# An early-fusion block on one Trainium2 core: the drain of a hand-ordered pipeline rewritten, more tile sets, and the last pair's norm in groups

## The chip, the core and the metric

The kernel runs on one NeuronCore of a Trainium2 chip. Five engines each have their own instruction stream and meet only at semaphores: PE (TensorE), DVE (VectorE), ACT (ScalarE), POOL (GpSimd) and SP (SyncE, which issues the DMAs here). The metric is device time of one execution in microseconds, the median of the runs. The kernel before took 1186.11 us, median of three runs from 1184.85 to 1186.3.

## The reference

The input is 32 images of 3x224x224 and 32 texts of 128x192. Each image becomes 196 tokens of 192 channels, beside one class token; with its text that makes 325 rows. Attention and a feed-forward network (FFN) follow. Cut to what matters:

```
def forward(x, ...):                                   # tokens of one image
    loc = dwconv(gelu(conv(x, pl_w, pl_b, stride=16)), pl_dw, pl_pw, pl_pwb)   # layer L
    g = gelu(conv(wavelet_packet(x), pg_w1, pg_b1))
    glob = conv(gelu(dwconv(g, pg_dw, pg_pw, pg_pwb)), pg_w2, pg_b2)           # layer G
    h = (1 - gate) * loc + gate * glob
    h = relu(dwconv(h, f1_...)); h = relu(dwconv(h, f2_...))                   # F1, F2
    t = layernorm(dwconv(loc + h, f3_...)) * ln_g + ln_b                       # F3
h = concatenate([cls, t, txt])                         # 1 + 196 + 128 rows of 192
n = layernorm(h)
q, k, v = (gelu(n @ w1 + b1) @ w2 + b2 for each of the three)
s = q @ k.T / SCALE * mask          # row i sees rows i-63 .. i; no softmax
h = h + layernorm(s @ v) * ln_w + ln_b
def bitlinear(x, w, g):             # x to 8 bits per row, w to -1, 0, 1
    x = rmsnorm(x, g); return round8(x) @ ternary(w).T
up, gate = split(bitlinear(layernorm(h), w_in, g_in))  # 192 -> 2 x 512
h = h + bitlinear(silu(gate) * up, w_out, g_out)       # 512 -> 192
```

Here dwconv is a depthwise 3x3 convolution followed by a matrix over the channels.

## The kernel before

Two images form a pair, and 16 pairs, 0 to 15, flow through a software pipeline of 23 turns (lines quoted are those of the kernel before). In turn `it` the engines embed pair it-1, compute its layers L, F1 and F2 as pair it-2, its F3 and token norm as pair it-3, the attention inputs as pair it-4, the attention's output norm and the FFN's input scales as pair it-5, and FFN tiles as pairs it-6 and it-7. A function `turn` for each engine lists the steps by hand, in one order for all turns; in the turns at the end, flags (`on[...]`) drop the steps for which no pair is left, and what is left keeps its order. An engine takes its instructions strictly in that order.

A depthwise layer is split by channels: nine taps over one part of them on DVE (L1349, L1359), nine products on ACT (L953) and their sums on POOL (L1905 to L1923) for the rest, then matmuls on PE (L474 to L479; for F3 L706 and L708). `add_loc` (L1378) takes F2's result and makes the input of F3; `token_biased` (L1389) takes F3's result. Attention has transposes on PE, six MLP layers (L528 to L539), scores, and products with the values; then the output norm of pair f: statistics on DVE (`output_bn`, L1439), six centred tiles on ACT (`output_norm`), one product and one sum over all tiles on POOL (`output_gain`, L1943; `output_add`, L1952).

The FFN works on tiles of 128 rows, five per pair; pairs 11 and 15 have a sixth with the rows left over. The steps of a tile, in order: transposes on PE (L627), copy to `xq` on ACT (L1016), hidden matmuls into two PSUM banks `up` and `gate` on PE (L638), tanh on ACT (`gate_tanh`, L1022), two products on DVE (`gated`, L1524, and `lifted`, L1544), the gain on POOL (L1889), a sum of squares on ACT, a maximum and five small instructions on DVE (`hidden_round`, L1308 to L1321) with a root on POOL (L1894, L1882), rounding on ACT (`round_hidden`, L1002), four transposes on PE (L648), copy to `yq` on ACT (L1010), the output matmuls on PE (L658), one instruction into `o_sb` on DVE (`finished`, L1534) and a store from SP.

Two PSUM banks and one set of scratch (`th`, `ya`, `y_f`, `yg` and so on) serve all tiles in turn; only for the last pair, `side(f, n)` gives odd tiles a second set, whose banks and memory earlier stages have left by then:

```
return n % 2 if last(f) else 0
```

`ffn_in` waits until DVE has read the previous tile's two banks, and until the tile before that has its output. `o_sb` has two buffers. The attention scratch and `x_sb`, `w_emb` and `early` are reused as tile scratch at the end, so rows of the trace name a tile's `ya` or `s` by the tensor whose memory it takes.

The steps of other lines that the prediction names: input layer norm on ACT (L967), token layer norm (DVE L1389 to L1398 and POOL L1985, L1995), the FFN's input gain on DVE (`token_gain`, L1490) and input rounding on ACT (L996).

Of the kernel before, what the change touches and what calls it, by code (L numbers as in the profile page):

```python
# [9 lines left out]
ALU = mybir.AluOpType  # L10
# [105 lines left out]
def stores_before(g, parity):  # L116
    return 16 * sum(stores_of(*TILE_LIST[i]) for i in range(parity, g, 2))


def side(f, n):  # L120

    return n % 2 if last(f) else 0


def alone(f, n):

    return last(f) and n > 0


def build(nc, xt, txt, cls, squares, f3w, v2w, plw, w1w, haar, cols, broads, gout, win, wout, mask,  # L130
          ident, out):
    ctx = ExitStack()
    with ctx:
# [80 lines left out]
        dq2 = [sb(f"dq2_{i}", [P, 1]) for i in range(2)]  # L214
        o_sb = [sb(f"o_sb{i}", [P, D]) for i in range(2)]
# [9 lines left out]
        ups, gts = [pUP, pA], [pGT, pB]  # L225
# [4 lines left out]
        ths, yas, yfs, sqs = ([a[:, :], x_flat[:, i * HID:(i + 1) * HID]] for i, a in enumerate((th, ya, y_f, sq_f)))  # L230
        ygs, r2s = ([a[:, :], e_flat[:, i * HID:(i + 1) * HID]] for i, a in enumerate((yg, r2)))
        xqs = [xq[:, :, :], e_flat[:, 2 * HID:2 * HID + P].bitcast(BF16).rearrange("p (c n) -> p c n", c=2)]
        yqs = [yq[:, :, :], e_flat[:, 2 * HID + P:2 * HID + 3 * P].bitcast(BF16).rearrange("p (c n) -> p c n", c=4)]
        s2s = [s2[:, :], e_flat[:, 2 * HID + 3 * P:2 * HID + 3 * P + 8]]
# [33 lines left out]
        y_scaled, h2_ready = sem("y_scaled"), sem("h2_ready")  # L268
        f1s = sem("f1s")
# [7 lines left out]
        stored = [sem("stored0"), sem("stored1")]  # L277
# [87 lines left out]

        CELLS = [(img, t, (P, ROWS[2])[t]) for img in range(2) for t in range(2)]
# [16 lines left out]
        def _(sp):  # L383
# [6 lines left out]
            def store(f, n):  # L390
                at = tile_no(f, n) % 2
# [14 lines left out]
            def join(f, par):  # L406
                sp.wait_ge(h2_ready, f + 1)
# [59 lines left out]
        def _(pe):  # L467
# [149 lines left out]
            def rounded_token_transposes(f, n):  # L617
# [13 lines left out]
            def ffn_in(f, n):  # L631
                m, s = rows_of(f, n), side(f, n)
                pe.wait_ge(f_xq, tile_no(f, n) + 1)
                if not (first(f) and n < 2 or alone(f, n)):
# [17 lines left out]
            def ffn_out(f, n):  # L652
                m, s = rows_of(f, n), side(f, n)
                pe.wait_ge(f_yq, tile_no(f, n) + 1)
                if not (first(f) and n == 0 or alone(f, n)):
# [209 lines left out]

            pe.wait_ge(s_early, ALL_EARLY)
# [13 lines left out]
            all_turns(turn)  # L880
# [3 lines left out]
        def _(act):  # L884
# [119 lines left out]
            def rounded_hidden(f, n):  # L1004
                m, s = rows_of(f, n), side(f, n)
                act.wait_ge(f_tr2, tile_no(f, n) + 1)
                if not (first(f) and n == 0 or alone(f, n)):
# [64 lines left out]
            def turn(it, par, on):  # L1072
# [80 lines left out]
                if on[5]:  # L1153
                    output_norm(it - 5, 0)
# [6 lines left out]
                if on[5]:  # L1161
                    output_norm(it - 5, 1)
# [120 lines left out]

            act.wait_ge(s_early, ALL_EARLY)
# [7 lines left out]
            all_turns(turn)  # L1292
# [3 lines left out]
        def _(dve):  # L1296
            v = nc.vector

            def hidden_round(j, f, n, par):
# [4 lines left out]
                if j == 0:  # L1304
                    dve.wait_ge(f_yg, tile_no(f, n) + 1)
                    if not (first(f) and n == 0 or alone(f, n)):
# [212 lines left out]

            def gated(f, n):  # L1520
# [6 lines left out]
            def finished(f, n):  # L1527
# [3 lines left out]
                at = tile_no(f, n) % 2  # L1531
                if not (first(f) and n < 2):
# [650 lines left out]
```

## Time and profile before

| what | value |
|---|---|
| median of three runs | 1186.11 us |
| profiled execution, own time | 1183.86 us |
| its span in the trace | 1182.1 us |
| mean granted TensorE clock | 0.94 of full |
| PE busy | 1056.5 us (89%) |
| DVE busy | 968.8 us (82%) |
| ACT busy | 883.8 us (75%) |
| POOL busy | 796.2 us (67%) |

The span runs from the first to the last instruction or transfer of the profiled execution; 1.76 us of its own time lie around it. Shares of busy time are means over the ramp, the steady turns and the drain, which differ. A line number in a row is one of the kernel before; a clock of 1.00 is full speed of TensorE. A row says which engine, the line, the operation, and out<-in by the program's names.

### The profile page before, as it was taken

Reading aid. Unit: us, or ns where it says so; the run is one execution under the profiler, and the core shown is the slowest. Engines: PE = TensorE matmul, PEld = TensorE weight load, DVE = VectorE, ACT = ScalarE, POOL = GpSimd, SP = SyncE. Lnnn points to the kernel's source line nnn. Section 1 sums busy time; section 2 is a strip of 40 time slices with the busy share of each in tenths; the row PEclk is TensorE's granted clock in tenths of the full one; section 3 lists DMA queues with packets and bytes.
Section 4 is the critical chain, followed back from the end, with each engine's and each line's share of the span. In section 5 each row is a group of like instructions: output and inputs, shape, how many; then the busy total and the mean of one; then the engine's idle time right before and its main releaser. Section 6 shows DMA issues by size and latency. Waiting matters only on the chain. (4 is left out here: it accounts for less than half of the span.)

```text
span 1182.1 us, 18959 instructions
## 1 busy us (share of the span) xinstructions
PE 1056.5 (89%) x5594; PEld 701.3 (59%) x5594; DVE 968.8 (82%) x2799; ACT 883.8 (75%) x2179; POOL 796.2 (67%) x913
## 2 busy tenths in 40 slices
PE   6886999999999999999999999999999877868434
PEld 4664676767666666767575757576766545444211
DVE  1678778989999999999898989899999976754543
ACT  4455767898979797979798988889897856654433
POOL 4246467778787878777877877787878755653422
PEclk9797999999999999999999999999999988979655
DMA  8111010101010101011010101010100000000000
GB/s 331 42 48 41 1 49 3 52 9 59 10 59 7 58 4 64 4 28 41 19 49 12 55 10 59 10 58 11 58 10 18 10 16 5 23 4 17 4 19 15
DMA packets 23686, 41.14 MB, mean 35 GB/s; under 512 B 3648, under 2 KB 20384, under 8 KB 21280
## 3 DMA queue, kind: packets, MB, share of 16 engines
q1 hardware_dynamic: 23584, 39.93, 10.0%
q8 instruction: 46, 0.75, 0.3%
q14 instruction: 56, 0.46, 0.1%
HBM read 31.02 MB, written 7.99 MB: 33 GB/s over the span
## 5 line engine op out<-in xcount | busy, mean ns | idle before, releaser
L1359 DVE SCALAR_TENSOR_TENSOR bank<-padA,c_col,bank 128x406 f32<-128x406 f32 x560 | 358.6, 640 | 9.1
L496 PE MATMUL bank<-x_sb,w_emb 128*128 128x392 f32 x576 | 221.3, 513 | 5.4 <-ACT padA L903 3.1
L953 ACT ACTIVATE prod<-padB,c_col 128x196 f32<-128x196 f32 x432 | 176.5, 451 | 7.2 <-DVE padB L1371 3.9
L1889 POOL TENSOR_TENSOR yg<-y_f,c_gout 128x512 f32<-128x512 f32 (+1 forms) x79 | 100.4, 1271 | 69.2 <-DVE y_f L1544 69.1
L496 PEld LDWEIGHTS bank<-x_sb,w_emb 128*128 128x128 f32 x576 | 102.5, 195 | 63.0 <-issue 12.8
L953 ACT ACTIVATE early<-padB,c_col 128x196 f32<-128x196 f32 x288 | 118.8, 449 | 3.7 <-POOL accB L1923 3.6
L1524 DVE SCALAR_TENSOR_TENSOR ya<-th,bank 128x512 f32<-128x512 f32 (+1 forms) x79 | 54.1, 684 | 56.4 <-ACT th L1022 55.2
L638 PE MATMUL bank<-w_in,xq 128*128 128x512 bf16 (+1 forms) x316 | 86.6, 399 | 8.8 <-ACT xq L1016 8.8
L1010 ACT ACTIVATE yq<-bank 128x512 bf16<-128x512 f16 (+1 forms) x79 | 46.8, 592 | 48.4 <-PE bank L648 47.2
L474 PE MATMUL bank<-accA,w_sq 128*128 128x196 f32 x256 | 67.6, 346 | 10.9 <-POOL accB L1923 6.8
L1022 ACT ACTIVATE th<-bank,sm 128x512 f32<-128x512 f32 (+1 forms) x79 | 53.7, 680 | 29.0 <-PE bank L638 29.0
L528 PE MATMUL bank<-xT,w_sq 128*128 128x325 f32 x192 | 65.7, 453 | 5.4 <-ACT hq L911 3.3
L1908 POOL TENSOR_TENSOR prod<-prod 128x392 f32<-128x392 f32 x48 | 48.8, 1016 | 28.8 <-ACT prod L953 28.7
L1905 POOL TENSOR_TENSOR prod<-prod 128x392 f32<-128x392 f32 x48 | 48.9, 1019 | 26.0 <-ACT prod L953 26.0
L1349 DVE TENSOR_SCALAR bank<-padA,c_col 128x406 f32<-128x406 f32 x80 | 51.0, 637 | 18.1 <-ACT padA L903 15.0
L475 PE MATMUL bank<-accB,w_sq 128*128 128x196 f32 x256 | 65.2, 337 | 0.0
L1002 ACT ACTIVATE r<-yg,s 128x512 f32<-128x512 f32 (+1 forms) x79 | 56.7, 718 | 10.7 <-DVE s L1321 10.6
L1943 POOL TENSOR_TENSOR y_sb<-y_sb,c_row 128x1152 f32<-128x1152 f32 x16 | 42.1, 2633 | 32.1 <-ACT y_sb L976 32.1
L1894 POOL TENSOR_SCALAR s<-s 128x1 f32<-128x1 f32 (+1 forms) x79 | 18.5, 235 | 65.2 <-ACT sq_f L1027 62.6
L638 PEld LDWEIGHTS bank<-w_in,xq 128*128 128x128 bf16 (+1 forms) x316 | 29.0, 101 | 52.6 <-ACT xq L1016 17.9
L967 ACT ACTIVATE xh<-h_sb,nm_a,rs_a 128x192 f32<-128x192 f32 (+1 forms) x144 | 60.1, 482 | 0.0
L648 PE MATMUL bank<-c_id,r 128*128 128x128 f16 (+1 forms) x316 | 32.8, 230 | 29.6 <-DVE y_f L1544 25.4
(276 smaller groups left out, 3030.9 us busy)
## 6 DMA issues: line engine op xcount, KB each, us to landing
x_sb<-xt SPq DMA_DIRECT2D x16, 1176.0 KB, 5.2
out<-o_sb SPq DMA_DIRECT2D x64, 96.0 KB
w_sq<-squares SPq DMA_DIRECT2D x1, 3840.0 KB, 16.4
h_sb<-txt SPq DMA_DIRECT2D x32, 51.8 KB
out<-o_sb SPq DMA_DIRECT2D x32, 48.0 KB
h_sb<-txt SPq DMA_DIRECT2D x32, 44.2 KB
w_in<-win SPq DMA_DIRECT2D x1, 1024.0 KB, 17.6
h<-h SPq DMA_DIRECT2D x16, 48.0 KB, 1.9
```

The costliest lines, as they stand in the source:

```text
L474: mm(dstA[img], w[:, AA, :], chunks[img], start=True, stop=False)
L475: done = mm(dstA[img], w[:, B0A + img, :], chunks[2], start=False, stop=True)
L496: done = mm(pE[:, 0:2 * N_PATCH], w_emb[:, k, m, :], x_sb[:, k, :], start=k == 0, stop=k == KC - 1)
L528: mm(dst[c], w[:, AA, :], src[:, c, :], start=True, stop=False)
L638: done = mm(dst[0:m, :], xqs[s][:, c, 0:m], w_in[:, c, half * HID:(half + 1) * HID], start=c == 0, stop=c == 1)
L953: made = go(grid(prod[ACC[s] ^ 1][:, k, :]), tap_view(padB[min(s, 2)], SIDE, k), ACT.Copy, scale=tapcol(s, 1, k))
L967: done = go(xh[0:m, t, at:at + hi - lo], h_sb[0:m, n, lo:hi], ACT.Identity, bias=nm_a[0:m, n:n + 1], scale=rs_a[0:m, n:n + 1])
L1002: go(r2s[s][0:m, :], ygs[s][0:m, :], ACT.Copy, scale=s2s[s][0:m, 6:7], bias=MAGIC_H).then_inc(r2_ready, 1)
L1022: go(ths[s][0:m, :], gts[s][0:m, :], ACT.Tanh, scale=sm[par][0:m, 2, n:n + 1]).then_inc(f_th, 1)
L1359: v.scalar_tensor_tensor(grid(acc if k == TAPS - 1 else run), tap_view(pad, ROWS_A, k), tapcol(s, 0, k), grid(run), ALU.mult, ALU.add).the ...
L1524: v.scalar_tensor_tensor(yas[s][0:m, :], ths[s][0:m, :], 1.0, gts[s][0:m, :], ALU.add, ALU.mult).then_inc(f_y, 1)
L1889: g.tensor_tensor(ygs[s][0:m, :], yfs[s][0:m, :], c_gout[0:m, :], ALU.mult).then_inc(f_yg, 1)
```

## The change

The list of turns ends early, after 17 turns on PE, ACT and SP and 16 on DVE and POOL, and each engine gets a function `drain()` that spells out all its remaining steps, one call a line, in a new order. Up to `finished(11, 0)` on DVE (912.84 us in the trace before) that order is the one of before.

Pairs 13 to 15 are the `TAIL`. `side` lets the tiles of pairs 13 and 14 alternate between two sets of banks and scratch, and those of pair 15 between three; the third set takes the banks pT[0], pT[1] and the memory of `hq`, `hk`, `hv`, `k2`, `xh` and `xT`. In the tail `ffn_in` waits only for the output of the tile that last had the same set. `o_sb`, and the semaphores of its stores, number three instead of two (`OUTS`), for all pairs.

The last pair's output norm and FFN scales are done in three groups of two tiles: statistics, then product and sum on DVE (`last_output`) in place of six instructions on ACT and two on POOL, then the FFN's input statistics, gain and scale, group by group; the roots stay on POOL. Tiles are rounded on ACT as their group is ready, and `join(15)` waits for two of the groups only.

```
+OUTS = 3
+TAIL = PAIRS - 3
 def side(f, n):
-    return n % 2 if last(f) else 0
+    if last(f):
+        return (n + 1) % 3
+    return (tile_no(f, n) - tile_no(TAIL, 0) + 1) % 2 if tail(f) else 0
...
-        ups, gts = [pUP, pA], [pGT, pB]
+        ups, gts = [pUP, pA, pT[0]], [pGT, pB, pT[1]]
...
+        OUT_GROUPS = (slice(0, 2), slice(2, 6, 3), slice(3, 5))
+        TOK_GROUPS = (slice(0, 2), slice(3, 5), slice(2, 6, 3))
...
-        def all_turns(turn):
-            for it in range(PAIRS + DEPTH - 1):
+        def all_turns(turn, stop):
+            for it in range(stop):
...
+            def drain():
...
+                rounded_token_transposes(15, 0)
+                rounded_token_transposes(15, 1)
...
-                if not (first(f) and n == 0 or alone(f, n)):
-                    pe.wait_ge(f_y, tile_no(f, n) * 2)
-                if not (first(f) and n < 2 or last(f) and n == 1):
-                    pe.wait_ge(f_out, tile_no(f, n) - 1)
+                if tail(f):
+                    if side_before(f, n):
+                        pe.wait_ge(f_out, side_before(f, n))
+                    elif side(f, n) == 1:
+                        pe.wait_ge(z_step, (PAIRS - 1) * 4 + 1)
+                    else:
+                        pe.wait_ge(at_act, PAIRS * ACT_UNITS)
+                else:
...
+            def last_output(f, par, j):
...
+                dve.wait_ge(l_root, j + 1)
+                for n in tiles_in(OUT_GROUPS[j]):
+                    m = ROWS[n % TILES]
+                    done = v.scalar_tensor_tensor(y_sb[0:m, n, :], y_sb[0:m, n, :], nm_y[0:m, n:n + 1],
+                                                  row("attn_ln_w", m), ALU.add, ALU.mult)
+                done.then_inc(l_y, 1)
+                dve.wait_ge(l_y, j + 1)
+                for n in tiles_in(OUT_GROUPS[j]):
+                    m = ROWS[n % TILES]
+                    done = v.scalar_tensor_tensor(h2[par][0:m, n, :], y_sb[0:m, n, :], rs_y[0:m, n:n + 1],
+                                                  hb_sb[0:m, n, :], ALU.mult, ALU.add)
+                done.then_inc(l_h2, 1)
...
+            def last_scale_0(f, par, j):
...
+                for n in tiles_in(TOK_GROUPS[j]):
+                    m = rows_of(f, n)
+                    done = v.bn_stats(st_f[0:m, n, :], joint(f, par, n))
...
+            def last_gain(f, par, j):
...
+                v.tensor_reduce(mx_f[:, q], w_g[:, q, :], AXX, ALU.max, apply_absolute_value=True).then_inc(l_f, 1)
...
-                at = tile_no(f, n) % 2
-                if not (first(f) and n < 2):
+                at = tile_no(f, n) % OUTS
+                if not (first(f) and n < OUTS):
```

The order is shown at three places. First POOL, around the last sum of layer F3 of the last pair (out `accB`, on which `token_biased` of pair 15 depends); `y_sb` and `h_1` are the output norm of pair 13, `yg` and `s` FFN tiles. Before:

```order
L1943 TENSOR_TENSOR y_sb<-y_sb,c_row 128x1152
L1952 TENSOR_TENSOR h_1<-y_sb,hb_sb 128x1152
L1905 TENSOR_TENSOR prod<-prod 128x392
L1889 TENSOR_TENSOR yg<-y_f,c_gout 128x512
L1908 TENSOR_TENSOR prod<-prod 128x392
L1911 TENSOR_TENSOR prod<-prod 128x392
L1914 TENSOR_TENSOR prod<-prod 128x196
L1894 TENSOR_SCALAR s<-s 128x1
L1882 TENSOR_TENSOR s<-s,c_mhalf 128x1
L1975 TENSOR_SCALAR sm<-mv_f 128x6
L1882 TENSOR_TENSOR sm<-sm,c_mhalf 128x6
L1923 TENSOR_TENSOR accB<-prod 128x196
```

After:

```order
L3017 TENSOR_TENSOR prod<-prod 128x392
L3020 TENSOR_TENSOR prod<-prod 128x392
L2998 TENSOR_TENSOR yg<-y_f,c_gout 128x512
L3023 TENSOR_TENSOR prod<-prod 128x196
L3067 TENSOR_TENSOR y_sb<-y_sb,c_row 128x1152
L3003 TENSOR_SCALAR s<-s 128x1
L2991 TENSOR_TENSOR s<-s,c_mhalf 128x1
L3076 TENSOR_TENSOR h_1<-y_sb,hb_sb 128x1152
L3032 TENSOR_TENSOR accB<-prod 128x196
```

Before, product and sum of pair 13's output norm stood ahead of all the sums of F3; now they stand between the sums of the products and the sum into `accB`, with a tile's root between them, and two instructions on `sm` (pair 13's FFN scales) are gone from there.

Second DVE, among the last pair's tiles (`x_sb`, `w_emb`, `k`, `hk` and `xT` stand for tile scratch). Before:

```order
L1524 SCALAR_TENSOR_TENSOR x_sb<-x_sb,bank 128x512
L1544 TENSOR_TENSOR x_sb<-x_sb,bank 128x512
L1534 SCALAR_TENSOR_TENSOR o_sb<-bank,dq_0,h_1 128x192
L1308 TENSOR_REDUCE w_emb<-w_emb 128x1
L1311 TENSOR_SCALAR w_emb<-w_emb,sm 128x1
L1314 TENSOR_SCALAR w_emb<-w_emb 128x1
L1317 RECIPROCAL w_emb<-w_emb 128x1
L1318 TENSOR_SCALAR dq_1<-w_emb,c_ws 128x1
L1321 TENSOR_SCALAR w_emb<-w_emb 128x1
L1524 SCALAR_TENSOR_TENSOR ya<-th,bank 128x512
L1544 TENSOR_TENSOR y_f<-ya,bank 128x512
L1534 SCALAR_TENSOR_TENSOR o_sb<-bank,dq_1,h_1 128x192
```

After:

```order
L2167 SCALAR_TENSOR_TENSOR x_sb<-x_sb,bank 128x512
L2187 TENSOR_TENSOR x_sb<-x_sb,bank 128x512
L2167 SCALAR_TENSOR_TENSOR k<-hk,bank 128x512
L2187 TENSOR_TENSOR xT<-k,bank 128x512
L2177 SCALAR_TENSOR_TENSOR o_sb<-bank,dq_0,h_0 128x192
L1855 TENSOR_REDUCE w_emb<-w_emb 128x1
L1858 TENSOR_SCALAR w_emb<-w_emb,sm 128x1
L1861 TENSOR_SCALAR w_emb<-w_emb 128x1
L1864 RECIPROCAL w_emb<-w_emb 128x1
L1865 TENSOR_SCALAR dq_1<-w_emb,c_ws 128x1
L1868 TENSOR_SCALAR w_emb<-w_emb 128x1
```

Before, each tile's two products were followed by the previous tile's output and its own maximum; now the products of two tiles, on two sets, stand in a row, then the output of pair 14's last tile, and only then the maximum of the first of the two.

Third PE, among the last pair's tiles (L627 and L638 are now L697 and L708, L648 and L658 now L718 and L728). Before:

```order
L627 MATMUL bank<-c_id,r 128x128 x2
L638 MATMUL bank<-w_in,w_emb 128x512 x4
L648 MATMUL bank<-c_id,r 128x128 x4
L658 MATMUL bank<-w_out,yq 128x192 x4
L627 MATMUL bank<-c_id,r 128x128 x2
L638 MATMUL bank<-w_in,xq 128x512 x4
L648 MATMUL bank<-c_id,w_emb 128x128 x4
L658 MATMUL bank<-w_out,w_emb 128x192 x4
```

After:

```order
L697 MATMUL bank<-c_id,r 128x128 x4
L708 MATMUL bank<-w_in,w_emb 128x512 x4
L708 MATMUL bank<-w_in,hq 128x512 x4
L718 MATMUL bank<-c_id,r 128x128 x4
L728 MATMUL bank<-w_out,yq 128x192 x4
L697 MATMUL bank<-c_id,r 128x128 x2
L708 MATMUL bank<-w_in,xq 128x512 x4
L718 MATMUL bank<-c_id,w_emb 128x128 x4
L728 MATMUL bank<-w_out,w_emb 128x192 x4
L697 MATMUL bank<-c_id,r 128x128 x2
```

Before, each tile's hidden matmuls were followed by the previous tile's transposes and output; now the input transposes of two tiles and their hidden matmuls stand in a row, and transposes and output of an earlier tile behind them.

## Rows read from the trace of the kernel before

**Rows 1.** The page: span; busy tenths and granted clock in 40 slices.
```profile
span 1182.1 us, 18959 instructions
...
PE   6886999999999999999999999999999877868434
...
PEclk9797999999999999999999999999999988979655
```

**Rows 2.** Busy by stretch: length, then busy us (instructions) of each engine, clock, DMA.
```profile
831.80:894.10 62.30, 61.62 (x345) 41.24 (x344) 58.98 (x175) 53.95 (x134) 49.26 (x56) 1.00 0.10 33
912.80:1182.10 269.30, 181.47 (x948) 110.69 (x946) 166.36 (x546) 150.58 (x346) 132.21 (x151) 0.79 0.05 13
1022.70:1101.80 79.10, 61.57 (x341) 37.93 (x337) 42.81 (x151) 41.24 (x93) 31.98 (x36) 0.89 0.05 14
1108.50:1182.10 73.60, 28.05 (x114) 11.05 (x114) 32.49 (x102) 28.55 (x60) 25.02 (x30) 0.50 0.05 14
```

**Rows 3.** What DVE waited for, 912.8 to 1182.1: total, times, longest.
```profile
DVE ya L1524 <- ACT th L1022: 34.7, 13, 7.2
DVE o_sb L1534 <- PE bank L658: 21.3, 13, 2.9
```

**Rows 4.** Timeline of DVE, four places: start, us, line, op, out<-in.
```profile
912.84 0.42 DVE L1534 SCALAR_TENSOR_TENSOR o_sb<-bank,dq,h 128x192 f32<-128x192 f32 x1
...
1004.07 0.75 DVE L1378 SCALAR_TENSOR_TENSOR padA<-bank,c_gate,locA 128x196 f32<-128x196 f32 x2 [0.98 <-PE bank L479]
...
1022.67 1.15 DVE L1389 TENSOR_TENSOR z_tok<-bank,c_row 128x192 f32<-128x192 f32 x4 [0.63 <-PE bank L708]
...
1101.81 0.61 DVE L1439 BATCH_NORM_STATS2 st_y<-y_sb 128x6 f32<-128x192 f32 x2
```

**Rows 5.** The chain of waits: hidden-layer tiles of the last pair on PE: start, us, what.
```profile
1132.82 1.90 PE bank L638 x4
...
1137.02 0.60 PE bank L648 x4
...
1138.29 0.82 PE bank L658 x4
...
1167.95 1.91 PE bank L638 x4
```

**Rows 6.** Timeline: first transpose of the last pair; the end.
```profile
1131.95 0.40 PE L627 MATMUL bank<-c_id,r 128*128 128x128 f16 x2 [10.48 <-ACT r L996]
...
1177.58 0.41 DVE L1534 SCALAR_TENSOR_TENSOR o_sb<-bank,dq,left 40x192 f32<-40x192 f32 x1 [2.38 <-PE bank L658]
1178.02 2.65 SPq L396 DMA_DIRECT2D out<-o_sb  x8
```

**Rows 7.** DVE groups from 860 us: shapes, count, busy us, mean ns, idle before.
```profile
L1308 DVE TENSOR_REDUCE s<-yg 128x1 f32<-128x512 f32 (+1 forms) x27 | 18.3, 679 | 3.9 <-POOL yg L1889 3.9
L1524 DVE SCALAR_TENSOR_TENSOR ya<-th,bank 128x512 f32<-128x512 f32 (+1 forms) x26 | 17.8, 684 | 36.5 <-ACT th L1022 36.5
L1534 DVE SCALAR_TENSOR_TENSOR o_sb<-bank,dq,h 128x192 f32<-128x192 f32 x28 | 11.6, 413 | 19.1 <-PE bank L658 19.0
L1311 DVE TENSOR_SCALAR s<-s,sm 128x1 f32<-128x1 f32 (+1 forms) x27 | 5.5, 205 | 6.3 <-POOL s L1882 6.3
```

**Rows 8.** The page: POOL's product of the output norms.
```profile
L1943 POOL TENSOR_TENSOR y_sb<-y_sb,c_row 128x1152 f32<-128x1152 f32 x16 | 42.1, 2633 | 32.1 <-ACT y_sb L976 32.1
```

**Rows 9.** The chain of waits: two MLP layers of the last pair.
```profile
1058.73 2.51 PE bank L528 x4
1061.24 1.43 PE bank L530 x4
...
1067.68 1.11 PE bank L528 x4
1068.79 0.80 PE bank L530 x4
```

**Rows 10.** All instructions of line 1490: ns min/median/max, first and last start.
```profile
L1490 DVE SCALAR_TENSOR_TENSOR w_g<-h,mv_f,c_row x80: 406/416/1164, 199.5 to 1127.4; 128x192 f32<-128x192 f32 x80
```

More of the change, by code:

```diff
@@ L116, in stores_before, with tail, side_before @@
 def stores_before(g, parity):
-    return 16 * sum(stores_of(*TILE_LIST[i]) for i in range(parity, g, 2))
+    return 16 * sum(stores_of(*TILE_LIST[i]) for i in range(parity, g, OUTS))
+TAIL = PAIRS - 3
+def tail(f):
+    return f >= TAIL
 def side(f, n):
-    return n % 2 if last(f) else 0
-def alone(f, n):
-    return last(f) and n > 0
+    if last(f):
+        return (n + 1) % 3
+    return (tile_no(f, n) - tile_no(TAIL, 0) + 1) % 2 if tail(f) else 0
+def side_before(f, n):
+    return max((i + 1 for i in range(tile_no(f, n)) if side(*TILE_LIST[i]) == side(f, n)), default=0)
 def build(nc, xt, txt, cls, squares, f3w, v2w, plw, w1w, haar, cols, broads, gout, win, wout, mask,
@@ L460, in _ @@
             sp.wait_ge(s_zero, N_ZERO)
-            all_turns(turn)
-            for parity in range(2):
+            all_turns(turn, 17)
+            drain()
+            for parity in range(OUTS):
                 sp.wait_ge(stored[parity], stores_before(len(TILE_LIST), parity))
@@ L633, in ffn_in @@
                 pe.wait_ge(f_xq, tile_no(f, n) + 1)
-                if not (first(f) and n < 2 or alone(f, n)):
+                if not (first(f) and n < 2 or tail(f)):
                     pe.wait_ge(f_yq, tile_no(f, n) - 1)
@@ L654, in ffn_out @@
                 pe.wait_ge(f_yq, tile_no(f, n) + 1)
-                if not (first(f) and n == 0 or alone(f, n)):
+                if not (first(f) and n == 0 or tail(f)):
                     pe.wait_ge(f_out, tile_no(f, n))
@@ L879, in _ @@
             pe.wait_ge(s_foldev, KC)
-            all_turns(turn)
+            all_turns(turn, 17)
+            drain()
         @block.scalar
@@ L1006, in rounded_hidden @@
                 act.wait_ge(f_tr2, tile_no(f, n) + 1)
-                if not (first(f) and n == 0 or alone(f, n)):
+                if not (first(f) and n == 0 or tail(f)):
                     act.wait_ge(f_o, tile_no(f, n))
@@ L1305, in hidden_round @@
                     dve.wait_ge(f_yg, tile_no(f, n) + 1)
-                    if not (first(f) and n == 0 or alone(f, n)):
+                    if not (first(f) and n == 0 or tail(f)):
                         dve.wait_ge(r2_ready, tile_no(f, n))
@@ L1540, in lifted @@
                 dve.wait_ge(f_y, tile_no(f, n) * 2 + 1)
-                if not (first(f) and n == 0 or alone(f, n)):
+                if not (first(f) and n == 0 or tail(f)):
                     dve.wait_ge(f_yg, tile_no(f, n))
@@ L1871, in _ @@
             assert gsteps[0] == GATE_STEPS
-            all_turns(turn)
+            all_turns(turn, 16)
+            drain()
         @block.gpsimd
@@ L1886, in hidden_scale @@
                 pool.wait_ge(f_y, (tile_no(f, n) + 1) * 2)
-                if not (first(f) and n == 0 or alone(f, n)):
+                if not (first(f) and n == 0 or tail(f)):
                     pool.wait_ge(r2_ready, tile_no(f, n))
```

1295 lines of the change are left out of this document (1262 added, 33 removed).

## The prediction

> **What bounds the kernel now.** I read the page's busy slices first [rows 1]: PE stands at nine tenths at a clock of nine from slice 5 to 31, and then both fall together. So there are two regimes, and busy time by stretch [rows 2] gives each its limit. In a steady turn of 62.3 us PE is busy for 61.62 and DVE for 58.98: nothing can be taken out there without taking work out. In the last 269.3 us (from 912.8) DVE is busy for 166.36, that is 62%, PE for 181.47 at a mean clock of 0.79, and the last 73.6 us run wholly at 0.50, which is 1.2 GHz. No engine bounds the drain; it is a chain of hand-offs. DVE's waits [rows 3] show of what kind: 34.7 us for the tanh of the next FFN tile (13 times, once 7.2) and 21.3 us for its output matmuls. Four places on DVE mark the stages [rows 4]: `finished(11, 0)` at 912.84, `add_loc(15)` at 1004.07, `token_biased(15)` at 1022.67, and the first statistics of the last pair's attention output at 1101.81. The last pair's tiles start with the transposes at 1131.95 [rows 6]; their hidden matmuls run from 1132.82 to 1167.95 [rows 5], six tiles, thus (1167.95 - 1132.82) / 5 = 7.03 us apart, and the last `o_sb` is written at 1177.58 to 1177.99. The change has the same order as before up to 912.84, so I sum from there.
>
> **The change part by part.**
>
> *To `add_loc(15)`, 91.2 us before.* The new order moves this step forward, ahead of FFN tiles that used to stand before it. What DVE does in this stretch now is a steady turn's set less one tile (maximum 0.679, two products at 0.684, output 0.413, five small ones at 0.205: 3.49 us [rows 7]), plus about a dozen statistics instructions at 0.31 (0.61 for two [rows 4]), 3.7. That is 62.3 + 0.2 = 62.5. DVE gets a new wait: the third statistics of pair 13's attention output stand right ahead of `add_loc(15)`, and their product on PE stands behind layer F2 of pair 15. Queued behind it on DVE are `add_loc(15)` and the nine taps of F3, for which PE and POOL wait. Its price lies between 0 and the longest wait of DVE in the drain, 7.2 [rows 3]; I take 3.5, about the middle and near the mean of those 13 waits (2.7). 912.8 + 62.5 + 3.5 = 978.8.
>
> *To `token_biased(15)`, 18.6 before.* Nine taps, nine products and the sums on POOL. Product and sum of pair 13's output norm, 2.63 each (the one at 2633 ns [rows 8], the other taken as alike), now stand before the last sum of F3 instead of before the first. They fill time in which POOL waited for products, or push the sum back by up to 5.3. I take 1.4 of it, since ACT's products are still the later input for most of the stretch: 20, bounds 18.6 and 23.9. 978.8 + 20 = 998.8.
>
> *To the first statistics of the last pair's output, 79.1 before.* The work is the same set of eight tiles' hidden matmuls, scores and attention MLPs, plus one MLP layer of pair 14, that is two of the 1.91 us (1.11 + 0.80) [rows 9]. At the mean clock of 0.89 [rows 2], 22% of 79.1, 17.4 us, ran at half speed; at full speed PE's 61.57 would be 61.57 - 17.4 / 2 = 53 us, with the added layer 57. That is the floor; the ceiling is 79.1. What brings it near the floor is that pair 13's tiles alternate between two sets, so the tile's chain (tanh, products, maximum, rounding) no longer stops the next tile's hidden matmuls. I take 57 + 9 for hand-offs of the last pair's attention, whose steps depend on each other: 66. 998.8 + 66 = 1064.8.
>
> *To the output of pair 14's fourth tile.* From here DVE is the fullest engine. Five tiles at 3.49 are 17.4 us. The norm and scales of the last pair come in three groups; each has four statistics (1.2), six products and sums of the kind of line 1490 at 0.416 [rows 10] (2.5), one maximum (0.5, an estimate below the 0.679 of a larger one) and about ten small ones at 0.2: 6.2 a group, 18.6 for three. ACT loses six instructions and POOL two, which are not late here. With 1 us of waiting this makes 37.0, bounds 33 (small ones overlapped) and 48 (30% waits): 1101.8. The two-input instructions are the place for a rule that speaks against the change. In line 1490, which has both inputs in SBUF, the median of 80 is 416 ns beside a minimum of 406, with POOL busy 49.26 of 62.3 us; only the worst took 1164 [rows 10]. So I add nothing.
>
> The Trainium skill ("SBUF — State Buffer", section Who interferes with whom) says that a DVE instruction with two SBUF inputs contends with a GpSimd instruction that reads SBUF, and that the later one blocks fully. By it, twelve new instructions at up to 1.164 - 0.416 = 0.75 more would cost 9 us; the row agrees in its maximum alone.
>
> *To the last output.* One tile alone takes 1132.82 - 1131.95 = 0.87 and 1177.99 - 1167.95 = 10.04, thus 10.9 us [rows 5, 6]. The other five follow at a distance that three sets no longer fix at 7.03: PE needs 0.40 + 1.90 + 0.60 + 0.82 = 3.72 a tile at the low clock [rows 5, 6], DVE 3.49. I take 4.6, PE's need and 0.9 for hand-offs: 23 + 10.9 = 33.9, bounds 5 x 3.49 + 10.9 = 28.4 and 5 x 7.03 + 10.9 = 46.1. 1101.8 + 33.9 = 1135.7. The store after it takes 1182.1 - 1178.0 = 4.1 [rows 1, 6]: 1139.8 for the span.
>
> *Without a term.* Three `o_sb` in the steady turns: PE is busy 61.62 of 62.3 there, so a turn can gain 0.7 at most, and I take 0. SP's `join(15)`, ahead of pair 14's stores, waits for two groups; three buffers cover some 3 x 4.6 = 14 us of that.
>
> The profiled execution took 1183.86, 1.8 over its span; so 1141.6 stands beside it. The median of the runs is 2.25 higher: 1143.9, and I say 1144.
>
> **The rivals.**
>
> *Dense drain.* DVE keeps the share of the steady turn, 58.98 / 62.3 = 94.7%. Its 166.36 us and some 8 more (twelve instructions at 0.416 and the grouped small ones) need 174.4 / 0.947 = 184 us: 1096.9, plus 10.9 + 1 for a last tile's chain, 4.1 and 4: 1117. For it speaks that the order was free to be chosen; against it, the last pair's chain, F1 to F3, norm, attention, which has to run in sequence with one pair's work left to lie beside it.
>
> *Waits handed on.* In-order lists wait at every place where one engine is later than the list supposed. My sum means DVE at 174.4 / 227 = 77%; halfway back to 62% is 69%: 174.4 / 0.69 = 253, span 1165.8, 1170 on the median's scale. For it speaks the new wait ahead of `add_loc(15)`; against it, that the lists before had just such waits.
>
> *No gain.* The waits are only moved to later places, and what stays within 0.2% (2.4 us, about what a measurement of this kernel can tell from no change) is 1184 to 1188.5. DVE's 56 us of waits for FFN tiles in the drain [rows 3] would have to stay as they are, on two and three sets.
>
> *Slower: PE falls to the low clock in the stage to 1064.8.* At present the clock is 0.89 there because PE has work in long runs [rows 2]. Lists that interleave short pieces leave PE gaps. The low level is there in the trace already: the last 73.6 us, at 0.50, in which PE waits for other engines most of the time (busy 28.05) [rows 2]. One MLP layer's half took 2.51 + 1.43 = 3.94 at the low level against 1.91 at the full one [rows 9], 2.06 times. With all 57 us of PE's work at that price the stage is 117 instead of 66, and the kernel 1195. It becomes slower than before once some 40 of these 57 us run low (1144 + 40 x 1.06 = 1186). Against it: with more sets PE has more to do at a time, not less.
>
> The Trainium skill ("TensorE: Matmul & The Clock Gate", section What's actually happening) says that the throttled state is the default and that activity releases it; the last 73.6 us agree, at 0.50 with PE busy 28.05 of them.
>
> **How the numbers follow.** Forecast 0.58 (its own range 1128 to 1160: the bounds of the terms above are 11 below and 38 above when all fall together, half of that when they don't); dense drain 0.20 (1106 to 1128); waits handed on 0.14 (1160 to 1182); no change 0.02; slower 0.06. The range 1114 to 1172 leaves out a third of the dense case, a third of the waits case and the last two: about 0.19. Faster: 0.58 + 0.20 + 0.14 = 0.92; same 0.02; slower 0.06.
>
> **What would show it.** Right: 912.8 unmoved within 2 us; `add_loc(15)` near 979 with a DVE wait for mixed products of 2 to 5 us just before it; `token_biased(15)` near 999; a clock of 0.95 or more in the stage after it, and 60 to 72 us for that stage; DVE at 85% or more in the group stage, its two-input instructions at a median under 0.45; last tiles 4 to 5.5 us apart, still at 0.50. Wrong: a clock of 0.5 through the attention of the last pair; two-input instructions near 0.8 or more; tiles still 7 us apart, waiting for tanh; POOL's last F3 sum more than 4 us behind the last product; any change in the steady turn.

## The result and the profile after

The changed kernel takes 1147.16 us, median of four runs (1145.75 to 1147.35), beside 1185.48 us for the kernel before on the same chip (1184.0 to 1186.3): a ratio of 0.9676, 95% interval 0.9659 to 0.9692. The profiled execution took 1147.02 us with a span of 1145.2. The forecast was 1144, from a span of 1139.8.

The page of the kernel after (span, then PE's busy tenths and granted clock in 40 slices):

```profile
span 1145.2 us, 18869 instructions
...
PE   6887999999999999999999999999999989868745
...
PEclk9888999999999999999999999999999999999855
```

The slices of 0.8 and 0.7 that stood ahead of the last three [rows 1] are gone; behind the ramp, no slice lies under 0.9 but the last three. The four places on DVE, and the last pair's first transposes, last output and store (timeline of the kernel after: start, us, engine, line, operation, out<-in):

```profile
977.93 0.73 DVE L1925 SCALAR_TENSOR_TENSOR padA<-bank,c_gate,locA 128x196 f32<-128x196 f32 x2
...
998.72 0.62 DVE L1936 TENSOR_TENSOR z_tok<-bank,c_row 128x192 f32<-128x192 f32 x2 [0.85 <-PE bank L778]
...
1072.86 0.36 DVE L2077 BATCH_NORM_STATS2 st_y<-y_sb 128x6 f32<-128x192 f32 x1 [0.31 <-ACT y_sb L1184]
...
1110.75 0.37 PE L697 MATMUL bank<-c_id,r 128*128 128x128 f16 x2 [0.60 <-DVE o_sb L2177]
...
1122.88 0.41 DVE L2177 SCALAR_TENSOR_TENSOR o_sb<-bank,dq,h 128x192 f32<-128x192 f32 x1
...
1140.80 0.41 DVE L2177 SCALAR_TENSOR_TENSOR o_sb<-bank,dq,left 40x192 f32<-40x192 f32 x1 [1.13 <-PE bank L728]
1141.23 2.64 SPq L418 DMA_DIRECT2D out<-o_sb  x8
```

`finished(11, 0)` starts at 914.0. Between these places lie the five stages of the sum (busy by stretch of the kernel after, columns as in [rows 2]: length, then busy us and instructions of PE, weight loads, DVE, ACT and POOL, clock, DMA share, GB/s; some matmul records are missing here):

```profile
912.80:977.90 65.10, 57.97 (x335) 42.25 (x337) 60.12 (x186) 51.18 (x127) 47.57 (x54) 0.97 0.04 11
977.90:998.70 20.80, 16.76 (x85) 8.21 (x87) 13.76 (x42) 16.61 (x41) 16.68 (x16) 1.00 0.04 10
998.70:1072.90 74.20, 58.63 (x358) 36.56 (x365) 49.63 (x179) 44.06 (x100) 35.76 (x42) 0.98 0.06 17
1072.90:1110.60 37.70, 17.06 (x78) 8.09 (x77) 31.21 (x114) 18.37 (x39) 15.27 (x25) 0.62 0.05 13
1110.60:1145.20 34.60, 19.63 (x90) 9.73 (x92) 20.54 (x62) 19.30 (x40) 14.08 (x21) 0.55 0.07 21
```

DVE is busy for 175.26 of 232.4 us, 75%, where it was 62% [rows 2]. Its waits (total, times, longest):

```profile
DVE o_sb L2177 <- PE bank L728: 11.8, 12, 2.0
DVE ya L2167 <- ACT th L1276: 8.3, 7, 2.0
DVE s L1855 <- POOL yg L2998: 6.9, 7, 1.4
DVE st_f L2011 <- DMA h<-h: 4.9, 2, 3.8
```

The 34.7 us for tanh and 21.3 for outputs [rows 3] have become 8.3 and 11.8; a wait of 3.8 for a transfer is new. These rows name only the tiles with scratch `ya`; with those whose scratch goes by the names `x_sb` and `k`, the waits for tanh are 41.3 us before and 10.9 after. The two-input instructions of the last norm (all of each line: ns minimum/median/maximum):

```profile
L2099 DVE SCALAR_TENSOR_TENSOR y_sb<-y_sb,nm_y,c_row x6: 405/410/842, 1081.8 to 1089.8; 128x192 f32<-128x192 f32 x4, 69x192 f32<-69x192 f32 x2
...
L2105 DVE SCALAR_TENSOR_TENSOR h<-y_sb,rs_y,hb_sb x6: 407/414/419, 1082.6 to 1090.5; 128x192 f32<-128x192 f32 x4, 69x192 f32<-69x192 f32 x2
```

One of twelve was long, by 0.43 us.

Read stage by stage, 26 of the 37 us were won before `add_loc(15)` (91.2 to 65.1 us). The experiments ask whether that is where they come from.

### The profile page after: what moved, and what is told of

It is laid out like the page before. It is cut to its first block, busy times and chain, and to the rows that moved or that the text cites. A ratio compares the mean times of both kernels' runs of the same rounds, so it can differ in the third digit from the quotient of the medians.

```text
span 1145.2 us, 18869 instructions
## 1 busy us (share of the span) xinstructions
PE 1042.2 (91%) x5546; PEld 693.6 (61%) x5594; DVE 976.7 (85%) x2829; ACT 882.1 (77%) x2173; POOL 791.2 (69%) x916
## 4 chain that ended last, share of the span: by engine, by line
PE 55%; ACT 22%; DVE 15%; issue 4%; POOL 2%; DMA 2%; SPq 1%; DVEq 0%; ACTq 0%; POOLq 0%
PE bank L558 10%; PE bank L590 4%; ACT xh L1218 3%; PE bank L708 3%; PE bank L592 3%; PE bank L601 3%; ACT y_sb L1227 3%; DVE bank L1906 3%; PE bank L600 3%; PE bank L652 3%; ACT early L1204 2%; PE bank L776 2%; PE bank L536 2%; PE bank L537 2%; PE bank L630 2%
## 5 line engine op out<-in xcount | busy, mean ns | idle before, releaser
L2998 POOL TENSOR_TENSOR yg<-y_f,c_gout 128x512 f32<-128x512 f32 (+2 forms) x73 | 92.9, 1272 | 49.0 <-DVE y_f L2187 48.7
L708 PE MATMUL bank<-w_in,xq 128*128 128x512 bf16 (+2 forms) x249 | 68.3, 390 | 8.0 <-ACT xq L1270 5.1
L2167 DVE SCALAR_TENSOR_TENSOR ya<-th,bank 128x512 f32<-128x512 f32 (+2 forms) x73 | 49.9, 684 | 29.8 <-ACT th L1276 28.7
L1276 ACT ACTIVATE th<-bank,sm 128x512 f32<-128x512 f32 (+2 forms) x73 | 49.7, 680 | 19.8 <-PE bank L708 19.7
L3067 POOL TENSOR_TENSOR y_sb<-y_sb,c_row 128x1152 f32<-128x1152 f32 x15 | 39.5, 2636 | 35.6 <-ACT y_sb L1227 35.6
L1264 ACT ACTIVATE yq<-bank 128x512 bf16<-128x512 f16 (+2 forms) x73 | 42.9, 588 | 24.0 <-PE bank L718 22.8
L1281 ACT ACTIVATE sq_f<-y_f,sm 128x512 f32<-128x512 f32 (+2 forms) x73 | 52.3, 716 | 11.3 <-DVE y_f L2187 11.1
L1256 ACT ACTIVATE r<-yg,s 128x512 f32<-128x512 f32 (+2 forms) x73 | 52.5, 719 | 9.9 <-DVE s L1868 9.8
L536 PEld LDWEIGHTS bank<-accA,w_sq 128*128 128x128 f32 x256 | 44.7, 192 | 19.6 <-issue 13.2
L1855 DVE TENSOR_REDUCE s<-yg 128x1 f32<-128x512 f32 (+2 forms) x73 | 49.5, 678 | 6.9 <-POOL yg L2998 6.9
## 6 DMA issues: line engine op xcount, KB each, us to landing
w_sq<-squares SPq DMA_DIRECT2D x1, 3840.0 KB, 15.6
```

What stands on the lines that cost most here:

```text
L536: mm(dstA[img], w[:, AA, :], chunks[img], start=True, stop=False)
L708: done = mm(dst[0:m, :], xqs[s][:, c, 0:m], w_in[:, c, half * HID:(half + 1) * HID], start=c == 0, stop=c == 1)
L1256: go(r2s[s][0:m, :], ygs[s][0:m, :], ACT.Copy, scale=s2s[s][0:m, 6:7], bias=MAGIC_H).then_inc(r2_ready, 1)
L1281: go(sqs[s][0:m, :], yfs[s][0:m, :], ACT.Square, scale=sm[par][0:m, 3, n:n + 1], accum_out=s2s[s][0:m, 0:1]).then_inc(f_ss, 1)
L2998: g.tensor_tensor(ygs[s][0:m, :], yfs[s][0:m, :], c_gout[0:m, :], ALU.mult).then_inc(f_yg, 1)
```

## The experiments

Each is compared with the kernel before as measured beside it, whose median lay between 1183.6 and 1184.4 us; so ratios are compared, and the changed kernel's is 0.9676.

**The new order alone, up to pair 12's last tile.** The kernel before; each engine takes its steps from the new lists up to a mark, and the rest in the order of before:

```
 # kernel before: one set (two for pair 15), two o_sb, whole norm
+ PE:   new list to ffn_in(12, 4)            + DVE:  to output_stats(14)
+ ACT:  new list to mixed_values_out(14, 2)  + POOL: to output_center(14)
  then: what is left, in the order of turn()
```

> The kernel before with the new order alone, up to the hidden matmuls of pair 12's last tile and the attention output of pair 14, and the order of before from there; one set of banks for pairs 13 and 14, two for pair 15, two output buffers, the old norm. Theory A (the order of the first 86 us is what gains): token_biased(15) stands near 999 to 1003 instead of 1022.7, and the end is early by most of that 20 to 24: 1160 to 1172. Theory B (the deferred tiles are only paid later, since one set lets them through 7 us or more apart, four to five tiles): token_biased(15) is early as well, but the end lies at 1178 to 1186.

Measured: 1194.02 us, ratio 1.009 (1.0069 to 1.0112): slower than before, and worse than either theory said. `token_biased(15)` did come at 1002.8, 20 us early. Its stretches from 912.8, with the same bounds as above:

```profile
912.80:982.00 69.20, 62.20 (x335) 45.85 (x336) 60.28 (x186) 51.36 (x127) 47.43 (x54) 0.90 0.04 10
982.00:1002.80 20.80, 16.78 (x85) 8.26 (x87) 13.76 (x43) 16.58 (x41) 16.70 (x16) 1.00 0.04 10
1002.80:1113.90 111.10, 73.71 (x393) 42.30 (x398) 58.90 (x205) 53.54 (x116) 41.56 (x50) 0.82 0.05 13
1113.90:1194.10 80.20, 31.99 (x132) 14.22 (x134) 36.17 (x120) 31.32 (x66) 27.03 (x33) 0.52 0.04 13
```

The third stage takes 111.1 us, where it took 79.1 before and 74.2 after the whole change. The early stages' gain is paid back there, and 12 us more with them. A gain read in a stage was a loan.

**Sets and buffers alone.** The changed kernel with the order of before in the drain and the old norm:

```
-  drain(): the new lists, groups for pair 15
+  drain(): the steps of turns 16/17 to 22 in their old order, whole norm
   # kept: side(), three sets, tail waits, OUTS = 3
```

> The changed kernel with the order of before in the drain and the old whole norm: what is left of the change is the two and three sets of banks and scratch and the three output buffers. After the first experiment (new order without sets: no gain). Theory A (the sets are what gains, since they take the 34.7 us of DVE's waits for tanh away): 15 to 30 us faster than before, 1155 to 1170. Theory B (in the order of before the engines reach the next tile too late to use a second set; order and sets gain only together): within 6 us of before, 1178 to 1186.

1162.81 us, ratio 0.9809 (0.9792 to 0.9825): Theory A by the time, with 59% of the whole gain at no change of order. Its reason holds in small part only. Waits for tanh, before (first two rows) and here:

```profile
DVE ya L1524 <- ACT th L1022: 34.7, 13, 7.2
DVE x_sb L1524 <- ACT x_sb L1022: 6.6, 3, 2.8
...
DVE ya L2164 <- ACT th L1271: 18.2, 8, 3.4
DVE x_sb L2164 <- ACT x_sb L1271: 14.5, 6, 4.7
DVE k L2164 <- ACT hk L1271: 2.0, 2, 1.4
```

That is 41.3 and 34.7 us: the sets alone take 6.6 of them, and the rest goes with the new order. The stretches, from 912.8 to `add_loc(15)`, to `token_biased(15)`, to the first statistics of the last pair's output, and to the end:

```profile
912.80:994.70 81.90, 65.09 (x397) 46.88 (x400) 73.44 (x233) 66.38 (x161) 59.09 (x71) 0.98 0.04 13
994.70:1013.30 18.60, 16.60 (x81) 8.01 (x82) 14.70 (x48) 12.37 (x29) 15.19 (x13) 1.00 0.05 14
1013.30:1088.00 74.70, 57.33 (x341) 35.86 (x343) 42.87 (x151) 41.12 (x93) 32.28 (x36) 0.95 0.05 15
1088.00:1160.50 72.50, 29.02 (x130) 13.01 (x130) 36.04 (x120) 31.18 (x66) 27.15 (x33) 0.55 0.05 14
```

`add_loc(15)` stood at 994.7 instead of 1004.1, before any tile uses a second set. The next one follows that up.

**The third output buffer alone.** The kernel before, with

```
-        o_sb = [sb(f"o_sb{i}", [P, D]) for i in range(2)]
+        o_sb = [sb(f"o_sb{i}", [P, D]) for i in range(3)]
 # and % 3 in place of % 2, three `stored` semaphores
```

> The kernel before with three output buffers and store semaphores, and nothing else of the change. In the run with the sets in the old order, add_loc(15) stood at 994.7 instead of 1004.1, ahead of any second set; the only other difference there is the third buffer, and in the trace of before DVE waits 4.0 us once for a store, at 964, with TensorE's clock at 0.5 from 968.6 to 982.2 behind it. Theory A (that wait and what follows it are the 9 us): add_loc(15) near 995, 5 to 10 us faster. Theory B (the 9 us are a variation of the clock between executions, or are given back later): within 3 us.

1173.8 us, ratio 0.9924 (0.9898 to 0.9949), `add_loc(15)` at 993.8: Theory A. In the trace of the kernel before, two waits on DVE (timeline), one on PE, and two stretches:

```profile
967.98 0.42 DVE L1534 SCALAR_TENSOR_TENSOR o_sb<-bank,dq,left 120x192 f32<-120x192 f32 x1 [4.04 <-DMA out<-o_sb]
...
980.44 0.22 DVE L1577 TENSOR_SCALAR r_key<-bank,c_qk 128x4 f32<-128x4 f32 x1 [7.01 <-PE bank L592]
...
968.54 0.36 PE L627 MATMUL bank<-c_id,r 128*128 128x128 f16 x2 [4.21 <-DVE o_sb L1534]
...
950.00:990.00 40.00, 30.36 (x162) 21.44 (x162) 25.08 (x87) 21.95 (x52) 19.31 (x23) 0.83 0.05 15
968.60:982.20 13.60, 13.12 (x57) 9.94 (x58) 5.11 (x17) 5.22 (x12) 6.20 (x7) 0.50 0.03 7
```

and the same stretch with three buffers:

```profile
950.00:990.00 40.00, 29.43 (x200) 20.79 (x200) 34.81 (x119) 31.32 (x75) 27.84 (x34) 0.99 0.06 16
```

DVE waits 4.04 us for a store; PE, which waits for DVE, stands idle for 4.21; then the granted clock is 0.50, the 1.2 GHz level, for 13.6 us, in which PE is busy for 13.12 and DVE waits another 7.01 us for PE's scores. A wait of 4 us cost 9 to 10. An estimate: at full clock the 13.12 us of matmuls would take about half [rows 9], 6.6 us less, so some 4 us are the wait itself and the rest is the clock. With a third buffer DVE's 25.08 us of work in these 40 us become 34.81, and nothing of it is given back later: the next two stages are 18.6 and 79.1 us in its trace, as before.

**Two output buffers in the new order.**

```
-OUTS = 3
+OUTS = 2
```

> The changed kernel with two output buffers and store semaphores instead of three. Theory A (a buffer is free long before it is wanted, except at the very end, where three tiles finish within 2.4 us and a store takes 4): 1 to 3 us slower, 1148 to 1150. Theory B (the 24 small stores of pair 11's last tile hold a buffer, and DVE waits for it in the middle of the drain): 4 to 8 us slower.

1145.6 us, ratio 0.969 (0.9668 to 0.9713): no difference. In the new order no store is waited for, at the end either; both theories were too high. The buffer and the order remove the same wait; nor does the first experiment, with two buffers and the early part of the new order, wait for a store.

**The early order with the sets.** The first experiment's lists, with sets and buffers as changed:

```
 # lists of the first experiment
-  TAIL sets, OUTS as before
+  side(), three sets, tail waits, OUTS = 3
```

> The first experiment's order (new up to the hidden matmuls of pair 12's last tile, then that of before), now with two and three sets, three output buffers, and the old whole norm. Theory A (the deferred tiles cost what they did for want of a set): most of the 47 us between the first experiment and the changed kernel comes back, 1150 to 1165. Theory B (the order of the later stages, in which the last pair's attention goes ahead of pair 13's tiles, is needed as well): 1175 to 1190.

1183.53 us, ratio 0.9999 (0.9986 to 1.0012): Theory B. Beside sets and buffers in the old order (0.9809) the early part of the new order loses 22 us; the later lists, in which the last pair's attention goes ahead of pair 13's tiles, turn that into a gain. Its third stage is as long as on one set (111.1):

```profile
998.10:1109.10 111.00, 76.10 (x398) 43.52 (x404) 58.60 (x204) 53.52 (x117) 41.56 (x50) 0.80 0.05 13
```

Stage by stage, what the whole new order adds to sets and buffers in the old order can be read from the traces: 81.9 us become 65.1 to `add_loc(15)`, 18.6 become 20.8 to `token_biased(15)`, 74.7 become 74.2 in the third stage, and from there to the end it is 72.5 and 72.3. In these last 72 us the new order finishes twelve tiles, the old one ten: the two that were put off cost nothing more there.

**The norm whole.**

```
-  DVE: last_output_stats, last_output, last_scale_0, last_gain, last_scale_1 (three groups)
+  DVE: output_bn, output_stats, hidden_bn, token_scale_0, token_gain, token_scale_1, token_scale_2
+  ACT: output_norm(15, 0), output_norm(15, 1)
+  POOL: output_center(15), output_gain(15), output_add(15, 1), token_root(15, 1)
```

> The changed kernel with the last pair's output norm, statistics and scales done whole, as before: six instructions on ACT, two on POOL, no product or sum on DVE; the rest of the order unchanged. Theory A (groups let the last pair's tiles start earlier): 3 to 8 us slower, 1150 to 1155. Theory B (DVE is the fullest engine in that stage, 29.5 of 35.6 us, and the groups load it with some 6 us more, while ACT and POOL idle): the same to 4 us faster, 1143 to 1147.

1148.67 us, ratio 0.9708 (0.9689 to 0.9728), the two-buffer kernel measured beside it at 0.969. That is 1.5 to 3 us slower than with groups, at the edge of what can be told, below Theory A's range and above Theory B's. The traces show no difference where the groups work: from the first statistics of the last pair's output to the end it is 72.3 us in both (1073.8 to 1146.1 here, 1072.9 to 1145.2 in the changed kernel). That the groups gain anything isn't shown.

**Two sets for the last pair**, its tiles in the order of before:

```
-        return (n + 1) % 3
+        return (n + 1) % 2
 # and the calls on pair 15's tiles in the order of before, in the places they had
```

> The changed kernel with two sets for the last pair instead of three, its tiles in the order of before on every engine; pairs 13 and 14 as changed. Theory A (three sets take the tiles from 7.0 us apart to 3.6): the last output comes 10 to 17 us later, 1157 to 1164. Theory B (the tiles were 7 us apart for the order, and the engines' work at the low clock sets the end): 0 to 6 us later.

1166.09 us, ratio 0.9844 (0.9829 to 0.9859): 19 us slower, a little above Theory A. The edit takes away a set and the order with it. First and last output of the pair in its trace:

```profile
1129.71 0.42 DVE L2177 SCALAR_TENSOR_TENSOR o_sb<-bank,dq,h 128x192 f32<-128x192 f32 x1 [1.38 <-PE bank L728]
...
1162.07 0.41 DVE L2177 SCALAR_TENSOR_TENSOR o_sb<-bank,dq,left 40x192 f32<-40x192 f32 x1 [2.38 <-PE bank L728]
```

That is 6.5 us a tile, against (1140.80 - 1122.88) / 5 = 3.58 on the mean; in the changed kernel the six outputs come in two bunches, from 1122.88 to 1129.29 and from 1138.43 to 1140.80. With three sets in the old order (sets and buffers alone) the outputs stand at 1126.8 to 1156.0, 5.8 apart: the third set itself gives less than the order that it allows.

**A transfer moved forward on SP.**

```
                 store(11, 4)
+                join(13, 1)
                 store(*last_tile(11))
-                join(13, 1)
```

> The changed kernel with one step moved on SP: the transfer that joins pair 13's text rows goes ahead of the 24 small stores of pair 11's last tile (991.3 to 999.4 in the trace), after which DVE waits 3.8 us for it at 1003.9. Theory A (the stage to the last pair's attention is long because DVE's waits are handed on to PE): 2 to 4 us faster, 1143 to 1145. Theory B (that stage is set by PE's and ACT's own chain): within 1 us.

1146.79 us, ratio 0.969 (0.967 to 0.971): Theory B by the time. DVE's wait for the transfer is gone, and the stage shrank from 74.2 to 73.3 us in the traces, at a mean clock of 0.93 instead of 0.98; so what the wait would cost at an even clock stays open.

**More work on one engine in the third stage**, one kernel each:

```
+ PE:  the four output matmuls twice, f in (12, 13)
+ ACT: go(junk[:, 0:m], up16[s][:, 0:m], ACT.Copy) ahead of the copy to yq, f in (12, 13)
+ DVE: v.tensor_reduce(junk1[0:m, n:n + 1], ygs[s][0:m, :], ...) ahead of the maximum, f == 12
```

> The changed kernel with the four output matmuls of every tile of pairs 12 and 13 issued twice, ten times some 0.34 us, 3.4 us of PE work between 1007 and 1081. Theory A (in the stage to the last pair's attention PE, busy for 58.7 of 74.3 us, is the bound, and its idle time is hand-offs that nothing fills): 2.5 to 4.5 us slower. Theory B (PE waits for others, and the extra work falls into its gaps): 0 to 1.5 us slower.

> The changed kernel with one more copy on ACT (128 columns into unused memory, about 0.27 us) ahead of the copy to yq, for the ten tiles of pairs 12 and 13: 2.7 us of ACT work between 1005 and 1080. Theory A (PE bounds that stage): 0 to 1.2 us slower. Theory B (the chain passes through ACT, which has its steps of tiles and attention in one queue): 1.5 to 3 us slower.

> The changed kernel with one more maximum on DVE (into unused memory, 0.68 us) ahead of each of the five maxima of pair 12's tiles: 3.4 us of DVE work between 980 and 1040. Theory A (PE bounds the stage): 0 to 1.2 us slower. Theory B (the chain passes through DVE, whose waits are handed on): 2 to 3.5 us slower.

Ratios: PE 0.9695 (0.9675 to 0.9716), ACT 0.9693 (0.9676 to 0.9709), DVE 0.9725 (0.9712 to 0.9738). Only DVE's interval lies clear of the changed kernel's: some 4 to 6 us for 3.4 us of work. So by the medians Theory B of the DVE run holds, with more than its range. The traces don't bear it out. The third stage in each of them, PE, ACT and DVE:

```profile
998.40:1078.00 79.60, 66.60 (x394) 43.83 (x400) 49.61 (x179) 44.00 (x99) 35.70 (x42) 0.89 0.06 16
...
998.90:1074.00 75.10, 60.90 (x364) 36.95 (x365) 49.73 (x178) 45.39 (x109) 35.66 (x42) 0.95 0.06 17
...
1000.40:1076.00 75.60, 60.28 (x364) 37.70 (x365) 52.15 (x182) 44.35 (x100) 35.67 (x42) 0.95 0.06 17
```

With the maxima the stage takes 75.6 us at a clock of 0.95, where the changed kernel has 74.2 at 0.98, and from `add_loc(15)` to the last output both take 162.9. The profiled execution with the maxima is the fastest of its five (1148.79), that with the matmuls the slowest of its four (1151.99). Medians and traces point to different engines, and the clock of the stage differs between executions, so which engine sets the length of this stage stays open.

**PE kept busy at the end.**

```
+            def warm():
+                for c in range(3):
+                    mm(pE[:, :], w_in[:, 0, 0:P], w_in[:, 0, 0:512], start=True, stop=True)
 # called behind the steps of PE's list after mixed_values(15, 2)
```

> The changed kernel with three matmuls of 512 columns into a bank that nothing reads, behind the steps of PE after the last pair's last product with its values (all but the input transposes of tiles); they compute nothing that is used. Theory A (from 1073 on the granted clock of 0.50 to 0.63 lengthens each tile's chain; kept busy, PE is granted more): clock above 0.85 there and 3 to 8 us faster, 1139 to 1144. Theory B (DVE sets the distance of the last tiles, 3.58 us against 3.49 of work, and matmuls ahead of real ones delay these): 0 to 5 us slower.

1148.7 us, ratio 0.9722 (0.9693 to 0.9751): not faster. Its last two stretches:

```profile
1073.00:1110.00 37.00, 23.22 (x111) 10.99 (x110) 30.25 (x111) 17.49 (x38) 14.41 (x25) 0.82 0.05 13
1110.00:1147.00 37.00, 26.86 (x156) 12.80 (x156) 20.94 (x62) 19.42 (x40) 14.29 (x21) 0.95 0.07 20
```

The clock rose from 0.62 and 0.55 to 0.82 and 0.95, and the time did not follow: Theory B by the time. Counted between the same steps of DVE, the two stages are 38.2 and 32.2 us, where they were 37.3 and 30.6. Of Theory B's two reasons the first fits the fourth stage, where DVE is busy for 31.21 of 37.7 us, but not the last. Between the first and the last output of the changed kernel DVE is busy for 11.50 of 17.9 us:

```profile
1122.90:1140.80 17.90, 11.10 (x57) 5.92 (x58) 11.50 (x37) 11.88 (x24) 8.22 (x12) 0.60 0.09 26
```

There the added matmuls, which stand ahead of real ones, may have cost what the clock gave; no run tells the two apart.

## Why the prediction was right, and where its reasons were not

The span came out 5.4 us over the sum of 1139.8, by terms that partly cancel. The start lay at 914.0, 1.2 late. *To `add_loc(15)`*: 63.9 against 66.0; the wait for the mixed product, priced at 3.5, is 1.32, with one of 1.97 for tanh just ahead of it. *To `token_biased(15)`*: 20.8 against 20. *To the first statistics*: 74.2 against 66. *To pair 14's fourth tile*: 37.7 against 37.0. *To the last output*: 30.5 against 33.9: the tiles stood 3.58 apart and not 4.6, which is 5.1 us less, and one tile alone took 1.7 more than the 10.9. The store: 4.0.

Two of these hits are luck. In the fourth stage the sum had 36.0 us of DVE work and 1 of waiting; DVE worked for 31.21 and stood idle for 6.5. In the second, 1.4 us of POOL's norm steps was taken "since ACT's products are still the later input". They are not:

```profile
984.26 0.80 ACT L1204 ACTIVATE prod<-padB,c_col 128x196 f32<-128x196 f32 x2
...
995.16 0.62 POOL L3032 TENSOR_TENSOR accB<-prod 128x196 f32<-128x196 f32 x1
...
995.93 0.40 PE L776 MATMUL bank<-w_f,accA 128*128 128x192 f32 x1 [0.23 <-POOL accB L3032]
```

POOL's last sum starts 10 us behind the last product, one of the prediction's own signs of being wrong. It cost PE 0.23 us all the same, since the steps ahead in PE's list lasted until 995.7.

The term that was mis-sized is the third, "57 + 9 for hand-offs". PE was busy for 58.63, near the floor of 57, at the clock that the prediction asked for (0.98); but it was idle for 15.6 us, 13 gaps of over 0.5 us among them, the longest 2.1. I took PE for the engine to count from. Whether it is, and how much of the 15.6 each engine's chain holds, stays open. The reason that more sets bring the stage near its floor is borne out in part: sets in the old order take it from 79.1 to 74.7, but with the early order alone it is 111 us with sets or without.

The reason that failed is the one for the first stage: that moving `add_loc(15)` ahead of tiles saves about 25 us. The length of the stage was nearly right; but some 10 of the 27 us saved are what the wait for a store buffer had cost. The prediction has this wait nowhere, and one more buffer removes it without any new order. And the move is worth something only with the rest: without the later lists it makes the kernel 22 us slower on three sets and 10 on one. Nor is the 0 for three `o_sb` right as it was argued, from steady turns: in the old drain the buffer is worth 0.76%, in the new one nothing. By ratios, with the parts put on one after the other: the third buffer takes the kernel to 0.9924, sets to 0.9809, the whole new order to 0.9708; the last step, groups to 0.9676, can't be told from nothing. Put on in another order, the parts would have other sizes.

The width was worked out wrongly: the bounds of the five terms add up to 23 us below and 44 above, not 11 and 38. Of the signs of being right, the start, both places after it, the clock of the third stage and the two-input instructions came out; the wait of 2 to 5 us (1.32), the stage of 60 to 72 us (74.2), DVE at 85% (83%) and the tiles 4 to 5.5 us apart at a clock of 0.50 (3.58, at 0.60) did not.

What was right besides: the steady turns unmoved; sets and order together take DVE's waits for tanh, 41.3 to 10.9 us; of the rivals, none came. *Dense drain* would have needed 94.7% on DVE, and it has 75%, near the 77% of the sum. *Waits handed on* shows in the new 3.8 us wait; moving the transfer made the stage about 1 us shorter. *Slower by the clock*: the stage ran at 0.98; but what that rival describes did happen in the kernel before, at 968.6, for a store, and the profiled run with more PE work had 0.89 and 79.6 us in the stage. The price of 9 us for two-input instructions did not come: their medians are 410 and 414 ns, and the one at 842 adds 0.43. The Trainium skill's rule ("SBUF — State Buffer", section Who interferes with whom) allows that one: it starts at 1089.00, while a product on POOL runs from 1088.29 to 1089.62. Beside the first eight of the twelve POOL stood idle, from 1080.7 to 1087.4, so the case says little on the rule's price.

## What to carry to other kernels

In a drain of in-order lists, a stage's gain is real only if the next stage can take the work that was pushed out of it; test a part of a change to the end of the kernel, not to the end of its stage. Before rewriting an order, look for the single wait that starts the trouble: a 4 us wait for a store buffer cost 9 to 10 us, by the estimate above more than half of it through PE's clock, and one more buffer of 128x192 removed it. Parts of one change may remove the same wait, so that each alone looks large or worthless according to what is there already.

## What the runs showed of the hardware

After PE had stood idle for 4.21 us, its granted clock was 0.50 for 13.6 us, though it was busy for 13.12 of them. Three matmuls of 512 columns behind each step raised the granted clock from 0.55 to 0.95 in the last stage. The first I had not expected from so short a stop. The Trainium skill ("TensorE: Matmul & The Clock Gate", section What's actually happening) has activity release the throttle; the second agrees. In the first, PE's work from 968.6 on did not bring the clock back before 982.2.

The same short stops need not cost the same. In the kernel after, PE stands idle for 1.45 us up to 1007.73 and for 2.06 up to 1010.07; in the profiled run with more PE work for 1.44 up to 1007.37 and 2.06 up to 1009.71. What follows, in the kernel after (two rows) and in that run:

```profile
1010.00:1016.00 6.00, 5.71 (x31) 4.43 (x33) 4.15 (x12) 1.47 (x4) 3.85 (x4) 0.72 0.02 5
1016.00:1022.00 6.00, 4.19 (x34) 2.60 (x32) 4.55 (x25) 1.77 (x4) 3.12 (x4) 1.00 0.00 0
...
1010.00:1016.00 6.00, 5.78 (x21) 4.35 (x22) 3.76 (x11) 1.11 (x3) 3.85 (x4) 0.50 0.02 5
1016.00:1022.00 6.00, 6.00 (x25) 4.44 (x25) 3.52 (x17) 0.81 (x2) 3.01 (x4) 0.50 0.00 0
```

PE was busy for 11.78 of these 12 us in that run and the clock stayed at 0.50. So stages of two executions compare only together with their clock.

The 24 stores of pair 11's sixth tile occupy SP's queue from 991.3 to 999.4 in the trace after, 0.34 us for each.
